# A two-layer cross-attention and mixture kernel on one core: bias product with 128 rows, second router with the batch's rows stationary, gate arithmetic in other instructions, calls reordered

## The reference, cut to what matters

```python
# layer 0: two attentions (char->sub, sub->char) with a sigmoid gate between them
x = x + tanh(g_xattn[0]) * L0_xattn(ln(x), ctx)
# layer 0 mixture: 8 experts, the best one of each row, its softmax weight as gate
x = x + tanh(g_ffn[0]) * L0_ffn(ln(x))
# layer 1: 16 heads of 16, rotary embedding, softmax, output product
x = x + tanh(g_xattn[1]) * (softmax(q @ k.T / 4) @ v @ Wo.T + bo)
# layer 1 mixture
logits = ln(x) @ w_gate.T                     # 256 x 8
vals, idx = top_k(logits, 2)
gates = zeros(256, 8).at[rows, idx].add(softmax(vals))
h = gelu(einsum('th,eih->tei', ln(x), w_fc))  # 8 experts, 128 hidden each
y = einsum('tei,ehi->teh', h, w_proj)
x = x + tanh(g_ffn[1]) * einsum('teh,te->th', y, gates)
```

## Time and profile before

| | |
|---|---|
| median of 3 runs | 615.13 us (613.02 to 617.68) |
| the profiled execution | 617.43 us, span 616.1 us |
| PE busy | 522.9 us (85%), 4068 matmuls |
| DVE, ACT, POOL busy | 378.4, 367.5, 296.0 us |
| mean granted clock of TensorE | 0.929 |

### The profile page before, as it was taken

One profiled execution on the slowest core, in us unless ns is written; L12 is line 12 of the kernel. 1 busy time (PEld: TensorE's weight loads), 2 busy tenths in 40 slices (PEclk: granted clock), 3 DMA queues, 4 the chain that ended last, 5 costly groups with the idle time before them and its releaser, 6 DMA issues.

```text
span 616.1 us, 11623 instructions
## 1 busy us (share of the span) xinstructions
PE 522.9 (85%) x4068; PEld 448.4 (73%) x4068; DVE 378.4 (61%) x946; ACT 367.5 (60%) x810; POOL 296.0 (48%) x370
## 2 busy tenths in 40 slices
PE   2898998999989978557868479899898997998877
PEld 2898898999989867336547248688695875776777
DVE  3755575647666774733525676777768577673454
ACT  4768658667485833122533376958567594666633
POOL 3245274351856335861613775837557282313144
PEclk9989999999999986757988689999899998998999
DMA  6181013274356546959894158081460906100000
GB/s 218 60 263 38 1 54 102 70 231 146 101 174 215 167 133 110 239 103 192 255 194 108 43 125 117 2 118 57 64 95 11 143 5 90 33 1 20 19 1 34
DMA packets 45597, 63.94 MB, mean 104 GB/s; under 512 B 6114, under 2 KB 31844, under 8 KB 45540
## 3 DMA queue, kind: packets, MB, share of 16 engines
q1 hardware_dynamic: 44004, 59.01, 40.7%
q0 software_dynamic: 1536, 4.20, 2.6%
HBM read 33.76 MB, written 12.45 MB: 75 GB/s over the span
## 4 chain that ended last, share of the span: by engine, by line
PE 43%; ACT 18%; POOL 13%; DVE 10%; issue 8%; DMA 6%; SPq 2%; POOLq 0%; ACTq 0%; DVEq 0%
PE psum L336 10%; PE psum L338 8%; PE psum L337 8%; PE psum L458 4%; ACT PT L1123 4%; PE psum L343 3%; PE psum L521 3%; DMA xs<-slots_d 2%; ACT xn L976 2%; DVE mpad L1699 2%; POOL slots_d L2153 2%; PE psum L510 2%; PE psum L495 1%; POOL rstd L2076 1%; ACT L1123 1%
## 5 line engine op out<-in xcount | busy, mean ns | idle before, releaser
L1699 DVE TENSOR_REDUCE mpad<-psum 128x2 f32<-128x512 f32 x128 | 83.4, 685 | 29.7 <-PE psum L495 28.8
L1123 ACT ACTIVATE PT<-psum 128x512 f32<-128x512 f32 x128 | 71.9, 596 | 18.3 <-PE psum L510 17.9
L2126 POOL TENSOR_TENSOR wA<-stage,wA 128x512 fp32r<-128x512 f32 x32 | 41.1, 1283 | 80.9 <-ACT wA L1165 74.4
L495 PE MATMUL psum<-st 96*128 96x256 bf16 x256 | 49.0, 293 | 29.1 <-DVE mpad L1699 24.6
L1767 DVE SCALAR_TENSOR_TENSOR xall<-psum,gat,xall 128x256 f32<-128x256 f32 x112 | 47.1, 475 | 20.5 <-PE psum L338 20.3
L495 PEld LDWEIGHTS psum<-st 96*128 96x128 bf16 x256 | 21.5, 102 | 40.9 <-DVE mpad L1699 30.8
L458 PE MATMUL psum<-wt,xsT 128*128 128x256 f32 x148 | 44.2, 430 | 7.5 <-ACT xsT L1081 7.4
L2072 POOL TENSOR_SCALAR nm<-mv 128x2 f32<-128x2 f32 x32 | 7.3, 229 | 89.0 <-DVE mv L1494 88.1
L510 PE MATMUL psum<-st 99*128 99x256 bf16 x256 | 46.3, 283 | 2.7 <-ACT PT L1123 2.0
L1631 DVE TENSOR_TENSOR ys<-psum,wt 128x256 f32<-128x256 f32 x37 | 15.4, 420 | 43.4 <-PE psum L458 39.4
L336 PE MATMUL psum<-wB,wA 128*128 128x256 f32 x128 | 40.0, 312 | 0.6 <-DVE xall L1767 0.6
(11 more groups left out here) (265 smaller groups left out, 1885.6 us busy)
## 6 DMA issues: line engine op xcount, KB each, us to landing
wt<-exp_d SPq DMA_DIRECT2D x37, 384.0 KB, 3.4
st<-parts SPq DMA_DIRECT2D x96, 128.0 KB
stage<-mats_d SPq DMA_DIRECT2D x21, 256.0 KB, 3.8
xs<-slots_d SPq DMA_DIRECT2D x37, 128.0 KB, 3.2
y_d<-ys SPq DMA_DIRECT2D x37, 128.0 KB, 2.9
cx<-ctx_d SPq DMA_DIRECT2D x16, 256.0 KB, 3.2
qr<-qp SPq DMA_DIRECT2D x16, 256.0 KB
slots_d<-ys SPq DMA_DIRECT2D x2, 1664.0 KB, 10.1
```

Of the source, the lines that this page charges most:

```text
L495: last = e.matmul(o[:, t * 256:(t + 1) * 256], s[0:96, 0, h, t * 128:(t + 1) * 128], s[0:96, 1, h, :], start=True, stop=True)
L1123: e.activation(flat(PT[:, n % 6, :, :]), ps("ST", b, h), ACT.Exp, scale=0.25).then_inc(a_ST, 1)
L1699: e.tensor_reduce(mpad[:, :, h:h + 1], ps("max", b, h).rearrange("p (a n) -> p a n", a=2), AX, ALU.max, negate=True).then_inc(v_max, 1)
L2126: e.tensor_tensor(hlo[:, i, :], stage[:, n % 4, :], hh[:, i, :].bitcast(F32), ALU.subtract).then_inc(h_lo, 1)
```

## The change

- The tensors `neg1` and `bo_r` of the bias product get 128 rows instead of 2. The rows of `bo_r` past the second are set to zero by one more POOL memset at the start. The number of matmuls stays the same.
- `route_D` holds 128 rows of the batch stationary and moves 16 columns, the high and the low part of the router's weights side by side: eight matmuls instead of six. Its result has the rows of the batch on the partitions. `logits_D`, `top_D` and `lt` are gone, and DVE adds the high and the low part by a TENSOR_REDUCE where it copied.
- In `d_top` the difference of the two best logits, the second gate and the sum of the two gated one-hot rows are SCALAR_TENSOR_TENSOR. There are still five small instructions after the selection, and one semaphore wait fewer between them.
- The calls in the lists of all engines stand in another order.

```diff
-        bo_r = sb("bo_r", [2, 256], F32R)
-        neg1 = sb("neg1", [2, 128], F32R)
+        bo_r = sb("bo_r", [128, 256], F32R)
+        neg1 = sb("neg1", [128, 128], F32R)
...
             def route_D(b):
-                o = take("g", "rt", b, "D")
+                o = take("g", "top", b, "D")
                 w.wait_ge(v_xl["D"], b + 1)
                 w.wait_ge(*w_of("r"))
-                for k in range(2):
-                    last = mm3(o[:, 0:256], hl(base["r"], lambda a: a[:, k * 128:k * 128 + 128]),
-                               hl(x4, lambda a: a[:, k, :]), k == 0, k == 1)
-                last.then_inc(t_rt, 1)
-
-            def top_D(b):
-                o = take("g", "top", b, "D")
-                w.wait_ge(a_lt, b + 1)
                 for t in range(2):
-                    last = e.transpose(o[:, t * 8:t * 8 + 8], lt[0:8, t * 128:(t + 1) * 128], ident[0:8, 0:8])
+                    for k in range(2):
+                        for part in range(2):
+                            last = e.matmul(o[:, t * 16:t * 16 + 16], x4[part][:, k, t * 128:(t + 1) * 128],
+                                            wr[:, k, :, :].rearrange("p a e -> p (a e)"), start=(k + part == 0), stop=(k + part == 2))
                 last.then_inc(t_top["D"], 1)
...
-            def logits_D(b):
-                w.wait_ge(t_rt, b + 1)
-                w.wait_ge(t_top["D"], b)
-                e.activation(lt[0:8, :], ps("rt", b, "D")[0:8, 0:256], ACT.Copy).then_inc(a_lt, 1)
...
-                e.tensor_tensor(rsm[:, :, 0], mx8[:, :, 0], mx8[:, :, 1], ALU.subtract).then_inc(v_top["D"], 1)
+                e.scalar_tensor_tensor(out=rsm[:, :, 0], in0=mx8[:, :, 0], scalar=1.0, in1=mx8[:, :, 1],
+                                       op0=ALU.mult, op1=ALU.subtract).then_inc(v_top["D"], 1)
...
-                e.tensor_tensor(rsm[:, :, 3], tg[:, 3:4].broadcast_to([128, 2]), rsm[:, :, 2], ALU.subtract).then_inc(v_g2, 1)
-                w.wait_ge(v_g2, 4 * b + 1)
+                e.scalar_tensor_tensor(out=rsm[:, :, 3], in0=rsm[:, :, 2], scalar=-1.0, in1=tg[:, 3:4].broadcast_to([128, 2]),
+                                       op0=ALU.mult, op1=ALU.add).then_inc(v_g2, 1)
+                w.wait_ge(v_g2, 3 * b + 1)
                 e.tensor_tensor(oh1[:, :, :], oh1[:, :, :], rsm[:, :, 2:3].broadcast_to([128, 2, 8]), ALU.mult).then_inc(v_g2, 1)
-                w.wait_ge(v_g2, 4 * b + 2)
-                e.tensor_tensor(oh2[:, :, :], oh2[:, :, :], rsm[:, :, 3:4].broadcast_to([128, 2, 8]), ALU.mult).then_inc(v_g2, 1)
-                w.wait_ge(v_g2, 4 * b + 4)
+                w.wait_ge(v_g2, 3 * b + 3)
                 w.wait_ge(a_y, 2 * (b - 1))
-                e.tensor_tensor(gat[:, b % 2, :, :], oh1[:, :, :], oh2[:, :, :], ALU.add).then_inc(v_gatD, 1)
+                for t in range(2):
+                    last = e.scalar_tensor_tensor(out=gat[:, b % 2, t, :], in0=oh2[:, t, :], scalar=rsm[:, t, 3:4], in1=oh1[:, t, :],
+                                                  op0=ALU.mult, op1=ALU.add)
+                last.then_inc(v_gatD, 1)
...
                 if 1 <= k - 9 < NB:
-                    c_max(12, k - 9)
...
+                if 1 <= k - 9 < NB:
+                    c_max(12, k - 9)
```

More of the change, by code:

```diff
@@ new lines, in tensor_program @@
+                if k == 7:
+                    moe_T(17)
+                if 0 <= k < NB:
+                    scores(0, k)
+                if k == 9:
+                    ln_T("C", "all", 1)
+                if k == 10:
+                    moe_w(26)
+                if k == 7:
+                    moe_w(16)
+                if k == 11:
+                    moe_w(35)
+                    c_out(0)
+                if 1 <= k - 11 < NB:
+                    c_out(k - 11)
+                if k == 10:
+                    c_maxT(0)
@@ new lines, in tensor_program @@
+                if k == 5:
+                    moe_w(6)
+                if k == 9:
+                    rank(2)
+                if 0 <= k < NB:
+                    scores(1, k)
+                if k == 8:
+                    moe_w(21)
+                if 0 <= k - 12 < NB:
+                    d_up(1, k - 12)
+                if k == 4:
+                    moe_T(2)
+                if k == 6:
+                    moe_T(11)
+                if 0 <= k - 1 < NB:
+                    ln_T("B", "all", k - 1)
@@ L728, in tensor_program @@
                     moe_T(9)
+                if k == 4:
+                    moe_w(3)
+                if k == 7:
+                    moe_w(18)
+                if k == 10:
+                    moe_w(28)
+                    moe_T(29, "g")
+                    c_exp(4, 0)
+                if k == 5:
+                    moe_w(8)
                 if 0 <= k - 11 < NB:
                     ln_T("D", "g", k - 11)
+                if k == 9:
+                    c_max(4, 0)
                 if 1 <= k - 10 < NB:
@@ L781, in tensor_program @@
                 if k == 10:
-                    c_exp(8, 0)
+                    moe_T(31, "g")
+                if k == 9:
+                    c_max(6, 0)
+                if 1 <= k - 9 < NB:
+                    c_max(6, k - 9)
+                    c_max(7, k - 9)
                 if k == 9:
                     c_max(7, 0)
+                if 0 <= k < NB:
+                    PV(1, k)
+                if 1 <= k - 10 < NB:
+                    c_exp(7, k - 10)
+                if k == 10:
+                    c_exp(9, 0)
+                    moe_T(32, "g")
@@ L807, in tensor_program @@
                 if k == 6:
-                    moe_T(14)
+                    moe_w(13)
+                if k == 3:
+                    moe_w(0)
+                if 1 <= k - 10 < NB:
+                    c_exp(8, k - 10)
+                if k == 4:
+                    moe_T(5)
+                if 1 <= k - 9 < NB:
+                    c_max(8, k - 9)
+                if k == 5:
+                    moe_w(9)
                 if k == 9:
                     c_max(9, 0)
-                if 1 <= k - 9 < NB:
-                    c_max(8, k - 9)
@@ L830, in tensor_program @@
-                if k == 10:
-                    c_PV(1, 0)
-                if 1 <= k - 10 < NB:
-                    c_exp(9, k - 10)
-                if 1 <= k - 9 < NB:
-                    c_max(9, k - 9)
                 if k == 6:
@@ L1556, in pick @@
                 o = ps("top", b, name)[:, 0:16].rearrange("p (t e) -> p t e", e=E)
+                if name == "D":
+                    o = ps("top", b, name)[:, 0:32].rearrange("p (t a e) -> p t e a", a=2, e=E)
                 if name == "B":
@@ new lines, in vector_program @@
+                if 1 <= k - 10 < NB:
+                    head_max(7, k - 10)
+                    head_max(8, k - 10)
+                if k == 7:
+                    y_out(14)
+                if k == 10:
+                    head_max(7, 0)
+                if k == 11:
+                    y_out(31)
+                if k == 10:
+                    head_max(8, 0)
+                if 0 <= k < NB:
+                    proj_lo("qc", k)
+                if k == 0:
+                    w_lo("vs")
@@ L2249, in pool_program @@
                     scatter(0)
+                if k == 11:
+                    gather(4)
+                if k == 6:
+                    scatter(1)
+                if k == 0:
+                    w_lo("g1")
+                if k == 10:
+                    gather(3)
+                if k == 7:
+                    gather(1)
+                if 0 <= k + 1 < NB:
+                    ln_rstd("A", k + 1)
+                if 0 <= k - 1 < NB:
+                    ln_rstd("B", k - 1)
+                if k == 9:
+                    scatter(2)
                 if 1 <= k - 9 < NB:
```

1490 lines of the change are left out of this document (697 added, 793 removed).

## The result

The changed kernel took 609.28 us (median of 8 runs, 606.53 to 611.13), the kernel before 615.98 on the same chip (613.02 to 617.68): ratio 0.9889, 95% interval 0.9863 to 0.9916. The gain is 6.7 us where the steps promised 16.7. The time lies inside the range, near its upper end, and it is the second rival's time (608 to 609), not the forecast's.

What follows compares the result with a forecast made beforehand. TensorE's work and few waits were taken to bound 30-230 and 350-590 us, DMA landings and short chains 230-350. Terms 6.1 + 0.6 + 8 + 3 + 2 - 3 = 16.7 us gave 599 us, range 590 to 611.

Steps and rivals of the forecast that it cites:

- second rival: Waits of `c_max` and `On` become waits for ACT or DVE, leaving 6.7 of 16.7 us: 608 to 609, chance 0.17.
- The bias product: 16 bias matmuls on TensorE, with 128 rows instead of 2, each save 0.38 us: 6.1 us.
- The router: Last batch: TensorE no longer idles for `lt`, as ACT loses its copies: 0.6 us.
- The gate arithmetic and its new place: `d_top` about 1.0 us shorter, plus moved products, cut TensorE's `c_max` wait for `head_max`: 8 us of 11.0.
- The cover by moved products: Before `c_max(12)`: a moved `d_down` (0.7 us) and `c_PV` help cover the 1.70 us wait; part of the 8 us.
- The transposes of `On`: TensorE's wait for `On` shrinks as `normed` and `c_out` come earlier: 3 us of 6.3.
- The last tile: Products of tiles 34 and 35 now precede TensorE's 3.94 us wait for tile 36's landing: 2 us.
- Given back: In the period, ACT would have to deliver each `PT` on time out of two banks: 3 us taken off.
- if the wait for `mpad` stays at 11: Sign of a wrong mechanism: TensorE's wait in the period was to fall from 11.0 to near 3 us.
- if the gain lies before 300 us: Sign of a wrong mechanism: TensorE's idle time was to fall some 10 us between 350 us and the end.

Runs made afterwards that it cites:

- e10: Changed kernel with only the gate vector's two halves behind the `top_tanh` wait, earlier gate instructions reading PSUM or having one column: 599.68 us, ratio 0.9689.
- e1: The kernel before with only the bias product's tiles raised to 128 rows: 611.5 us, ratio 0.992.
- e4: The changed kernel in its new order, with the old five TENSOR_TENSOR gate instructions: 604.91 us, ratio 0.9835.
- e7: e1 with `c_out` moved ahead of `d_up(1)` on TensorE and `normed` ahead of `head_max(15)` on VectorE: 611.92 us, ratio 0.9926.
- e6: e4 with `c_max(12)` and `c_max(13)` moved behind `d_down(6)` on TensorE: 610.6 us, ratio 0.9901.
- e9: Changed kernel with one operand of each gate instruction behind the `top_tanh` wait read from PSUM, gates not computed, for time alone: 597.1 us, ratio 0.9659.
- e5: Changed kernel with gate halves made by `tensor_scalar` with per-partition scalars, one SBUF tensor per instruction: 618.39 us, ratio 1.0026.

## Why the prediction was wrong, step by step

- **The bias product**, 6.1: right at the instruction (0.12 us in front of all 16), 4 to 6 us at the end, since a wait follows some of them.
- **The router**, 0.6: right at its place, from its first matmul to the product behind it 0.91 us in the last batch instead of 1.71. But `d_top` of that batch is 2.75 us instead of 2.20, and from the last bias matmul to the end the two kernels differ by 0.3 us.
- **The gate arithmetic and its new place**, 8: this step failed. "What is won is a step of the chain" was the error. I had said that the new instructions are held like the old, and then let the second half of `gat` go free "behind one wait". POOL took its turn between the two halves (1.20 and 0.76 us), so the chain was not one hold shorter. The 0.57 us of `top_tanh` were also not there, because two `st_exp` had come ahead of it. `d_top` was to be 1.0 us shorter and came out 0.6 longer; at 4.2 us per microsecond, the clock with it, that is 6.7 us, two thirds of the 10 that are missing. e10 shows what the step was worth when it is done: with `d_top` at 4.41 us in batch 1, 1.2 shorter than before, the ratio is 0.9689, which is 597 against 615.98. That the forecast's 599 is near it is partly luck, since the last tile gave more there and `On` nothing.
- **The cover by moved products** was the other half of that step. The six periods of the two orders with nearly equal `d_top` are equal (203.8 in e1, 204.0 in e4), so at that length it was worth nothing in itself.
- **The transposes of `On`**, 3: 0. The wait is gone to the last 0.1 us, and e7 shows it coming back elsewhere by name. The row of 6.3 us was read as a price; it was a place in DVE's backlog.
- **The last tile**, 2: more than that. At the transposes of batch 1 the changed kernel is 6.5 us ahead, of which 1.2 were there at batch 0. From the one to the other it is 42 to 45 us in the kernels of the new order and 46 to 49 in those of the old. The wait of 3.94 us is gone, and so is a stretch of 6.8 us at 1.2 GHz that began beside it, at 317.5. I had said that the DMA is not earlier, and it hardly is (0.9 us), but what stood behind its wait took 5.5 us more, the slow stretch with it. A wait of 3.88 us for another DMA stands behind it now. No run moved this tile alone.
- **Given back**, 3: too small. Over the six periods the distances of more than 0.3 us between two matmul starts, each less the 0.11 us of neighbours, sum to 30.7 us before and 32.6 after, though 6.4 in front of the transposes of `On` are gone and so are 2.4 behind the bias matmuls. In their place: 2.3 more in front of `c_max` and `c_exp` behind a `c_PV` or one another, 2.4 in front of the same behind `d_up` and 1.3 behind `d_down`, 2.1 in front of the transposes of the maxima and 1.3 behind those of `c_out`, 1.9 between products of `c_PV`. The clock cost one stretch more than before in these periods (four against three), about 1.2 us by the estimate above, and it could have given: e10 has one.

In the terms of the sum, the six periods were to be 8 us shorter without the bias (8 + 3 - 3). They came out 4 us longer without it (207.9 against 203.8 in e1), and the tile stretch gave back some 4.5 of these 12. So the total fell on the second rival's time without its mechanism: the rival had nothing won but bias and last batch, and here a gain ahead of the periods paid for a loss in them.

I had named the sign to look for: "if the wait for `mpad` stays at 11" came true. The other, "if the gain lies before 300 us", came true in kind only, since the gain outside the bias lies before the periods, but most of it between 277 and 320 us. A small misreading besides: in the period ACT and DVE have 31% and 32% free, not a third or more.

## What to carry to other kernels

A short VectorE instruction between SBUF tiles beside a busy GpSimd can last as long as one GpSimd instruction (1.2 us here), each anew, so count them on the critical chain, and give them an operand in PSUM or a single column, or move them ahead of the wait. A wait that was removed by reordering was not won here (e6, e7), because the engine waited for had a backlog: look what stands next on that engine and price that first. Before adding up waits from the list, take the engine that they wait for and ask what shortens its own list.

## What the hardware showed beyond what I had expected

- With GpSimd busy, SCALAR_TENSOR_TENSOR, TENSOR_TENSOR and TENSOR_SCALAR between SBUF tiles of 2 to 16 columns took 0.6 to 1.3 us; the same with an operand in PSUM 0.16 to 0.23 (e9, e10), and TENSOR_SCALAR of one column 0.19 to 0.21 each (e5).
- Not every such instruction is held: L1741 (0.16 us) in the changed kernel started at 390.79, as the POOL instruction before it ended at 390.85 and the next began at 391.01.
- The four stops of TensorE of 2.03 to 2.65 us for `c_max(12)` in the changed kernel were each followed by 3.4 us at 1.2 GHz, as was the one of 2.16 us in the kernel before; of the four stops of 1.7 us in the kernel before two were (those that ended at 363.6 and 437.0) and two were not (400.6 and 474.6).
